# Cross-attention and FFN on one core: the join of four score minima moves from VectorE to GpSimd

## The reference

```python
x = x + xattn(layernorm(x), ctx, Wq, bq, Wkv, bkv, Wp, bp)
x = x + ffn(layernorm(x), w13, w2, norm_w)

# xattn: q, k per head and row, v per channel, are rounded to 8 bits (scale = absmax/127)
attn = softmax(q @ k.T)                       # over all 5776 keys
s    = max(attn over a row) / 255
attn = clip(round(attn / s), 0, 255) * s      # unsigned 8 bits, scale from the row's maximum
out  = (attn @ v) @ Wp + bp
# ffn: 8-bit rounding of the input, relu(x1)^2 * x3, RMS norm, 8-bit rounding, @ w2
```

## Time and profile before

| | us |
|---|---|
| median of 3 runs | 1847.6 (1844.59 to 1848.37) |
| profiled execution, its own time | 1847.68 |
| its span | 1845.9 |
| busy PE / VectorE / ScalarE / GpSimd | 1631.2 / 1691.0 / 1391.7 / 1375.3 |
| eviction L1295, 800 instructions without the accumulator reads | 1283.2, idle before it 20.5 |
| casts L1529, 400 | 1048.5, idle before them 223.6 |
| exponential L1088, 200 | 1041.2, idle before it 166.7 |

### The profile page before, as it was taken

The page is one execution under the profiler, slowest core; times in us unless marked ns, Lnnn a source line. Parts: engine busy times, 40 slices in busy tenths (PEclk is TensorE's granted clock), DMA queues, the critical chain, the costliest instruction groups (busy, mean ns, idle before and its releaser), DMA issues.

```text
span 1845.9 us, 41823 instructions
## 1 busy us (share of the span) xinstructions
PE 1631.2 (88%) x17032; PEld 1153.6 (62%) x17032; DVE 1691.0 (92%) x2670; ACT 1391.7 (75%) x1362; POOL 1375.3 (75%) x759
## 2 busy tenths in 40 slices
PE   7997899989888888888898898888889888789998
PEld 6884666666566666655566666555555555478876
DVE  6869999999999999999999999999999999986665
ACT  2446898888988898889888988897888888742232
POOL 1432789898879888888898889887898798753232
PEclk9999999999999999999999999999999999989999
DMA  5578988998899899989998998889888998732221
GB/s 175 193 224 201 209 187 177 184 196 166 181 186 198 176 193 184 187 164 177 191 200 177 181 196 170 158 158 181 168 169 157 205 185 160 166 116 45 67 58 47
DMA packets 851530, 309.96 MB, mean 168 GB/s; under 512 B 784966, under 2 KB 813964, under 8 KB 851212
## 3 DMA queue, kind: packets, MB, share of 16 engines
q1 hardware_dynamic: 851340, 307.29, 81.0%
HBM read 74.26 MB, written 39.59 MB: 62 GB/s over the span
## 4 chain that ended last, share of the span: by engine, by line
DVE 57%; PE 21%; issue 9%; POOL 7%; DMA 5%; ACT 1%; SPq 1%; POOLq 0%; DVEq 0%; ACTq 0%
DVE S L1295 51%; PE PS L876 5%; POOL PT L1529 5%; PE PK L913 3%; DMA PP<-Pr 3%; PE PS L743 2%; PE PK L682 2%; PE PK L684 2%; PE PS L711 2%; DVE MJ L1321 1%; PE PO L684 1%; DVE kam L1186 1%; PE PO L682 1%; DVE VMX L1190 1%; PE PO L762 1%
## 5 line engine op out<-in xcount | busy, mean ns | idle before, releaser
L1295 DVE TENSOR_SCALAR_CACHE_REDUCE S<-PS,SQN 128x1536 f32<-128x1536 f32 (+1 forms) x768 | 1283.2, 1714 | 20.5 <-PE PS L743 10.1
L1529 POOL CAST PT<-PP 128x3072 uint16<-128x3072 uint8 (+1 forms) x400 | 1048.5, 2650 | 223.6 <-DMA PP<-Pr 217.7
L1088 ACT ACTIVATE Pr<-S,MS 128x5888 uint8<-128x5888 f32 x200 | 1041.2, 5206 | 166.7 <-DVE MJ L1321 140.0
L743 PE MATMUL PS<-KT,QT 96*128 96x512 bf16 (+1 forms) x2496 | 633.4, 373 | 153.2 <-DVE S L1295 140.0
L762 PEld LDWEIGHTS PO<-VI,PT 128*128 128x128 f16 x9200 | 338.4, 96 | 199.6 <-issue 31.3
L743 PEld LDWEIGHTS PS<-KT,QT 96*128 96x128 bf16 (+1 forms) x2496 | 191.5, 99 | 364.9 <-DVE S L1295 131.1
L762 PE MATMUL PO<-VI,PT 128*128 128x32 bf16 x9200 | 356.3, 178 | 20.1 <-ACT AO L1038 9.7
L684 PE MATMUL PK<-CT,WG 128*128 128x128 f32 (+1 forms) x1288 | 212.7, 293 | 7.0 <-DMA CT<-ctxt 7.0
L682 PE MATMUL PK<-WG,CT 128*128 128x128 f32 (+1 forms) x1288 | 210.7, 293 | 6.3 <-ACT VF L949 3.7
L684 PEld LDWEIGHTS PK<-CT,WG 128*128 128x128 f32 x1288 | 169.1, 194 | 10.0 <-issue 7.8
L682 PEld LDWEIGHTS PK<-WG,CT 128*128 128x128 f32 (+1 forms) x1288 | 167.0, 192 | 8.5 <-issue 6.6
(11 more groups left out here) (156 smaller groups left out, 1538.0 us busy)
## 6 DMA issues: line engine op xcount, KB each, us to landing
CT<-ctxt SPq DMA_DIRECT2D x180, 256.0 KB, 3.2
k_rows<-KS SPq DMA_DIRECT2D x39, 512.0 KB, 4.0
q_rows<-QS SPq DMA_DIRECT2D x13, 512.0 KB, 4.6
W13F<-w13T SPq DMA_DIRECT2D x12, 352.0 KB, 3.7
PP<-Pr SPq DMA_TRANSPOSE x200, 6.0
XT<-x SPq DMA_DIRECT2D x12, 256.0 KB, 4.4
XR<-x SPq DMA_DIRECT2D x12, 256.0 KB, 3.3
base_rows<-XO SPq DMA_DIRECT2D x12, 256.0 KB, 3.3
```

Source lines behind the costliest of these rows:

```text
L743: last = pe.matmul(PS[n % 2][p0:p0 + r, f:f + w], QT[h % 3][0:PARTS * HD, q0:q0 + r], KT[h % 3][0:PARTS * HD, c * CHUNK + f:c * CHUNK + f ...
L1088: act.activation(Pr[i % 2].rearrange("p t q b -> p t b q"), S[i % 2].rearrange("p (t b q) -> p t b q", b=2, q=P), ACT.Exp, bias=MS[:, i % ...
L1295: v.tensor_scalar(S[i % 2][:, c * CHUNK:c * CHUNK + CW[c]], PS[n % 2][:, 0:CW[c]], neg_step, None, ALU.mult, ALU.min, accum_out=MN[:, i % ...
L1529: gp.tensor_copy(PT[i % 2][:, 2 * t0:2 * t1, :].rearrange("p (t b) q -> p t b q", b=2), PP[i % 2][:, t0:t1, :].bitcast(U8).rearrange("p t ...
```

## The change

VectorE no longer joins the minima. Evictions c = 2 and c = 3 take the minimum of eviction c - 2 as a further operand, so that their accumulators continue from it: MN[2] becomes the least of chunks 0 and 2, MN[3] the least of chunks 1 and 3. Ahead of these two VectorE waits for eviction n - 2 (`s_ev` >= n - 1). A new piece of work on GpSimd, `offset(i)`, waits for the four evictions of step i, takes the lesser of MN[3] and MN[2], adds log 255 and writes MS (`s_mx`). It is one tensor_scalar on one element per partition. Its due time is i + 0.5, so it stands between the two casts of tile i - 2. The buffer MJ goes.

```diff
                     v.wait_ge(M["s_qk"], n + 1)
-                    v.tensor_scalar(S[i % 2][:, c * CHUNK:c * CHUNK + CW[c]], PS[n % 2][:, 0:CW[c]], neg_step, None,
+                    if c >= 2:
+                        v.wait_ge(M["s_ev"], n - 1)
+                    least = MN[:, i % 2, c - 2:c - 1] if c >= 2 else None
+                    v.tensor_scalar(S[i % 2][:, c * CHUNK:c * CHUNK + CW[c]], PS[n % 2][:, 0:CW[c]], neg_step, least,
                                     ALU.mult, ALU.min, accum_out=MN[:, i % 2, c:c + 1]).then_inc(M["s_ev"], 1)
...
-                v.wait_ge(M["s_ev"], NC_ * (i + 1))
-
-                v.tensor_scalar(MJ[:, :], MN[:, i % 2, :], LN255, None, ALU.add, ALU.min,
-                                accum_out=MS[:, i % 2, 0:1]).then_inc(M["s_mx"], 1)
...
+            def offset(i):
+
+                gp.wait_ge(M["s_ev"], NC_ * (i + 1))
+                gp.tensor_scalar(MS[:, i % 2, 0:1], MN[:, i % 2, 3:4], MN[:, i % 2, 2:3], LN255, ALU.min,
+                                 ALU.add).then_inc(M["s_mx"], 1)
...
             todo += [(i + 2.3 + 0.4 * part, unpack, (i, part)) for i in range(NA) for part in range(NCAST)]
+            todo += [(i + 0.5, offset, (i,)) for i in range(NA)]
```

More of the change, by code:

```diff
@@ L226, in build @@
         MS = sb("MS", [P, 2, 1], F32)
-        MJ = sb("MJ", [P, NC_], F32)
         st = sb("st", [P, 2, 8], F32)
```

## The result

| | before | after |
|---|---|---|
| median | 1847.87 us (4 runs, 1844.59 to 1848.37) | 1963.97 us (4 runs, 1963.34 to 1966.42) |
| ratio | | 1.0627 (95% interval 1.061 to 1.0645) |
| span of the profiled execution | 1845.9 us | 1964.2 us |
| busy PE / VectorE / ScalarE / GpSimd | 1631 / 1691 / 1392 / 1375 | 1684 / 1694 / 1394 / 1447 |

The kernel is 116 us slower. The forecast was 1922 us, with a range from 1860 to 1985; within it the likeliest part was to be 1880 to 1950, and the result lies above that. VectorE's busy time is the same, GpSimd's grows by 71 us, 58 of them the 200 joins, and TensorE's by 53 us, at a lower mean clock (0.934 after, 0.982 before). What grew most is waiting.

What follows compares the result with a forecast made beforehand. VectorE's evictions were taken to set most attention steps. With a 15.0 us two-step loop, 90 intervals add 126 us and 31 add 24; 150 us over overlapping pairs is 75 us, giving 1922 us, range 1860 to 1985.

Steps and rivals of the forecast that it cites:

- The mechanism: Join queued behind GpSimd's first cast closes a two-step loop: exponential, transfer, cast, join, next exponential of the same parity.
- Second operand: VectorE's evictions three and four: another per-partition operand costs 0.06 us each, 0.12 us a step, 24 us in all.
- Join: On GpSimd: the small operation that joins the minima takes 0.25 us, one operand per partition.
- From the end of the cast to the exponential: GpSimd to ScalarE: join plus some 0.15 us for two hand-overs, 0.40 us from first cast's end to exponential's start.
- VectorE's added wait for an earlier eviction: Evictions three and four wait for the eviction before the previous one, which ended 1.7 us earlier: costs nothing.
- rival 1: Faster: VectorE stays the bound, as slower steps thin transfers and each lands in its minimum; 1833 or 1804 us; chance 0.12.
- The sum: Attention steps: 126 us plus 24 us over overlapping pairs is 75 us of time, so 1922 us.
- I take 15.0: Two-step loop through GpSimd: 14.65 us average over 89 first casts plus 0.40 gives 15.05; 15.0 us used for two steps.
- I set both equal: For the 77 long intervals, VectorE's 0.2 us a pair saved (15 us) is taken to cancel the transfer's scatter.
- Rival 3: Backlog persists: GpSimd idles ahead of the second cast, its backlog may grow; 15.6 us every pair, 1979 us; chance 0.17.
- One count: In 152 of 198 steps the first cast of tile i-2 ends after step i's last eviction.
- The signs that I named: If right: ScalarE's join wait over 200 us, VectorE's exponential waits over 100 places, intervals near 15, 0.22 us gap gone.

Runs made afterwards that it cites:

- the wait alone: Kernel before plus one line: ScalarE's exponential of step i also waits for the first cast of tile i-2; 1920.68 us, ratio 1.0395.

## Why the prediction was right, and where its size was off

**The mechanism** holds at each step. The join is late because it is queued behind the first cast; the wait alone makes 72 us, the same instructions in other places 27 to 318 us over before, and the same work without the dependency 3 us.

**The prices.** Second operand: 0.06 us forecast, 1.875 against 1.815 measured. Join: 0.25 forecast, 0.288 measured. From the end of the cast to the exponential: 0.40 forecast, 0.42 measured. VectorE's added wait for an earlier eviction: no such wait stands in its list, as forecast. The transfer got hardly shorter with the slower steps (5.9 us to landing in the median, 6.0 before), which was the hope of rival 1.

**The sum** was 75 us and the result is 116. Its classes, with the means of the same intervals in both traces, taken from the start of a step's first eviction to that of the next step but one (half of the sum is time):

| two-step intervals of before | before | forecast | after | forecast, us | measured, us |
|---|---|---|---|---|---|
| 90 short | 13.60 | 15.0 | 15.21 | 63 | 72 |
| 31 between | 14.22 | 15.0 | 15.57 | 12 | 21 |
| 77 long | 15.33 | 15.33 | 15.84 | 0 | 20 |

The classes make 113 of the 116 us, 38 more than forecast. Two terms were too small, and each makes about half of that.

The first is the loop's length, "I take 15.0". It came from the steps in which the first cast waited for a transfer issued on time, and every step counts. In after the way from the exponential's start to the end of its first cast averages 14.97 us over all 200 steps (15.20 in before), and 14.91 over the 198 that have a next exponential but one. With the 0.42 us behind the cast that is 15.33, and the sum by it is (90 x 1.73 + 31 x 1.11) / 2 = 95 us. One rule for both traces (transfer issued within 5.4 us of the exponential's start, GpSimd idle ahead of the cast) gives 93 steps with a mean of 14.35 us in after and 107 others with 15.51; in before it is 81 with 14.47, less than the 14.65 of the prediction, and 119 with 15.69. In the others the transfer is issued late, or GpSimd comes late to the cast: in 63 steps it starts over 0.3 us behind the landing, 91 us in total (before: 62 steps, 80 us).

The second is "I set both equal". Where the loop and VectorE are about as long, the time of a pair is the later of the two each time and not the later of their means. From the end of the first cast to the exponential the mean is 0.61 us and not 0.42, as in 44 of 198 steps something other than the cast came later; half of the 0.19 us in 198 steps is 19 us. Nine in ten loops lie between 13.5 and 17.1 us, and the long intervals rose by half a microsecond. No run changes this scatter alone, so this second half is read from the trace and not tested.

Rival 3 came nearer than the forecast: it had 15.6 us for every pair, and they average 15.5. Its 1979 us holds a slip: from 15.33 to 15.6 the long intervals rise by 0.27 and not by 0.5, which makes 1970. But its reason, a backlog of GpSimd that grows, is hardly seen, as the late casts were there before. The measured time lies in the wide range because that range was drawn to take in rival 3; the term that I summed with was too short. One count is also a little off, without a term that hangs on it: in before the first cast ends after the join's start in 161 of 198 steps, where the prediction has 152 against the last eviction.

Read as causes, the 116 us are 72 us of the wait alone, and some 34 us of the join inside the loop (0.34 us longer from cast to exponential than with the wait alone, 0.42 against 0.08, half of it in 200 steps; the run with the join done twice supports the half). Some 10 us are left. In the traces the loop up to the end of the first cast is 14.97 us in after and 14.85 with the wait alone, and half of that in 200 steps is 12 us; whether the operand, the held second cast or the interplay makes it, the runs do not tell.

**The signs that I named.** ScalarE's wait for the join above 200 us: 270. Few intervals at 13.4: 13 of 198 are under 13.7. The gap of 0.22 us gone: yes. Wrong was that VectorE would wait for the exponential in over 100 places with over 100 us: it was 62 and 71 us. Another 54 us more it waits for TensorE, which itself waits 111 us for ScalarE's copy of the values out of PSUM. That copy is queued behind the late exponential; that the one wait makes the other is my reading of the order, and no run tests it. I had named who waits behind the join on GpSimd, but not who waits behind the exponential on ScalarE.

**The join's price.** It took 0.288 us on GpSimd, the old one with four elements 0.157 us on VectorE, and the same two-operand one there 0.214 us, so for the same operation on both engines the factor is 1.35. By the factor of two of the Trainium skill (GPSIMD Engine Reference, Engine selection) an estimate from the old join is 0.31 us for it, with which the trace agrees roughly. The price of the operation was the small part.

**The clock.** The stretches at half clock went from 12 to 54 as TensorE's waits grew. The rule of the Trainium skill against long idle gaps (TensorE: Matmul & The Clock Gate, Why this matters for your kernels) agrees with that. No gain in time was seen from following it, in the run with the added matmuls.

## What to carry to other kernels

When a small operation moves to an engine with a fixed order, look first at what stands ahead of it and what that waits for. If it leads back to the operation's own consumer some steps ago, a loop is closed, and its length divided by the steps it spans is a floor for the step. Everything in it counts by that fraction: here half. Before the change is built, the wait alone can be put into the old kernel; here that one line showed 62% of the loss. Take the loop's length from all its rounds and not from the plain ones. Where it and the old bound are about equally long, add for their scatter, as the later of two counts each time.

## What the runs showed that I had not expected

TensorE's clock was at half for 262 of 1964 us (the sum of the 54 stretches); more matmuls took that to 104 us with the time unchanged. And a tensor_scalar of one element per partition on GpSimd took by its operands: 0.286 us with two from SBUF, 0.36 with three, where the 352-element one without any took 0.488.
